# First relational layer of a graph network: the row that is picked on TensorE becomes the last tile of the following, even chunk

## The chip, the cores and the metric

One NeuronCore of a Trainium2 chip runs the whole program. The metric is the device time of one execution in microseconds (us), lower is better. Times given as "median" are medians of separate executions; the rows of the trace come from one profiled execution.

## The reference

The program is a two-block graph network on 3125 nodes of 128 features and 100000 edges that are sorted by destination. The first block is relational (two layers), the second a GCN (two layers); both have a layer norm ahead and a residual around them. Cut to what matters here, a relational layer is:

```python
def _rel_layer(h, src, dst, etype, norm, V, comp, loop_w, bias, activation):
    c = comp[etype]                                   # 8 coefficients an edge
    for b in range(num_bases):                        # 8 bases
        xb = h @ V[b]
        m = m + c[:, b, None] * xb[src]
    m = m * norm
    agg = jax.ops.segment_sum(m, dst, num_segments=h.shape[0])
    out = agg + bias + h @ loop_w
```

Each edge needs the row `h[src]` of its source node, 128 floats, and the sum over the edges of a destination node. That fetch of rows is what the change is about.

## The kernel before, in words

The 100000 edges are cut into 782 tiles of 128 edges, eight tiles to a chunk (`CHUNK`), 98 chunks, four chunks to a group of 128 destination nodes (`CPG`), 25 groups. The first relational layer is "layer 0" in the code (`relational_layer(..., 0, ...)`), the second "layer 1". Both keep the rows of 64 tiles in a ring in SBUF (`ring`, eight chunks of eight tiles). The engines run their own queues, written out by hand and kept together by counting semaphores.

Of layer 0, chunk by chunk:

- **POOL** (GpSimd) gathers the rows of a tile with one indirect DMA (line 854 for chunks 2 to 7, line 831 for the rest), in the order of the tiles. Ahead of a chunk it waits for `edges_done` of the chunk four before (`LEAD`), half way through it for `product_done`. Every gather counts 16 onto `ring_even` or `ring_odd`, by the parity of its chunk; `landings` says how much has come when a chunk is complete, `gathers` how many of its tiles POOL fetches.
- **PE** (TensorE) has in a chunk: `sum_slab` (lines 1180, 1211, 1216, 1219), which waits for DVE's `rel_M` (line 983) and counts the graph's adjacency; 13 or 12 matmuls of the picked row in three parts (`pick_sixth`, line 1280), between them the 16 matmuls of the coefficients (line 483); then `sum_edges` and the eight matmuls of the chunk's tiles (line 1342; each stands as two records in the trace, since it is float32). The third part of the picked row's matmuls stands behind the fourth tile.
- **DVE** (VectorE) builds for each chunk the operands `rel_lo` (978), `rel_C` (993) and `rel_M` (983), the one-hot types of a later chunk (`make_onehot`, 474, two instructions) and the coefficients (489, 494). Once in a group it folds the adjacency into degrees (`fold_degrees`, 1061 to 1063).

One tile in every second chunk is not gathered: it is **picked on PE**. SP loads the 128 source numbers of the tile's edges into `src_row` (`load_sources`), DVE compares them with the node numbers into the one-hot `pick` (`make_pick`, 1016, in two halves), PE multiplies it with the node features, which lie in SBUF as three bf16 parts (`h_parts`), and DVE adds the three parts into the ring's slot (`keep_picked`, 1032), which counts `row_ready`. PE's matmuls of one picked row are spread over two chunks: the first half over an even chunk, the second over the odd chunk behind it. 46 rows are made so, in chunk pairs whose odd chunk is 5 to 95 (`first_picks`). Before the change the row is tile 7 of that same odd chunk, so PE waits for `row_ready` ahead of its last tile (line 1341):

```python
if layer == 0 and i == CHUNK - 1 and j % 2 == 1 and not (isinstance(c, int) and not first_picks(c)):
    pe.wait_ge(row_ready, number(g, j) + 1)
```

On DVE `keep_picked` stands in the queue behind `rel_M` of the *next* (even) chunk and ahead of the second half of the next pick. At the layer's end chunk 96 is followed by the turn of the last group (lines 563 to 565), `sum_slab` and the edges of chunk 97, and two degree sums on DVE (`sum_degrees`, line 1052). Then layer 1 starts, and with it POOL's next gather.

## Time and profile before

| what | value |
|---|---|
| median of 3 executions | 2001.1 us (1999.92 to 2003.72) |
| profiled execution, its own time | 1999.43 us |
| its span in the trace | 1997.8 us |
| layer 0's gathers on POOL end | 978.8 us into the span |
| layer 1's first gather starts | 999.6 us into the span |

Busy shares over the whole span: PE 86%, DVE 75%, POOL 69%, ACT 18%. The page of the profile gives the share of an engine's busy time, and in a second list what each engine waited for; the two differ where an engine has a fixed pause between two instructions, as POOL has here.

### The profile page before, as it was taken

The numbers are of one execution on the slowest core, as the hardware profiler recorded it, in microseconds if no ns is written. First come the engines' busy times: TensorE is split into PE (matmuls) and PEld (weight loads), VectorE is DVE, ScalarE is ACT, GpSimd is POOL, SyncE is SP. The second block draws the span as 40 slices with busy tenths as digits, with TensorE's granted clock in tenths as the row PEclk, the third lists the DMA queues.
The fourth block names the chain that finished last, engine by engine and source line by source line (L and its number), as shares of the span: only waits on it lengthen the run. The fifth ranks groups of instructions, "written<-read, shape, count | busy, mean of one in ns | idle before, by whom it ended". The sixth has DMA issues, their size and how long they took to land. (4 is left out here: it accounts for less than half of the span.)

```text
span 1997.8 us, 41905 instructions
## 1 busy us (share of the span) xinstructions
PE 1727.5 (86%) x12855; PEld 1237.7 (62%) x12856; DVE 1493.0 (75%) x2360; ACT 357.1 (18%) x869; POOL 1383.6 (69%) x1505
## 2 busy tenths in 40 slices
PE   1488888888888888888659999999999999999998
PEld 1366656556556556556537777767667676676564
DVE  7898888888888888887478888877777777652533
ACT  2032222222222222222201011101011010011300
POOL 5777777777777777777477777777777777777000
PEclk8589989889889889988779999999999999989999
DMA  5334334334334334333222222233333322325473
GB/s 151 92 98 114 96 99 109 94 98 110 94 97 108 95 97 109 95 96 88 70 60 64 63 64 64 63 85 86 86 101 93 86 80 80 115 57 167 154 240 120
DMA packets 196506, 196.71 MB, mean 98 GB/s; under 512 B 109132, under 2 KB 160089, under 8 KB 196410
## 3 DMA queue, kind: packets, MB, share of 16 engines
q0 software_dynamic: 45056, 92.36, 18.1%
q1 hardware_dynamic: 143302, 99.03, 17.2%
q10 hardware_dynamic: 8052, 4.04, 0.7%
q8 instruction: 59, 0.97, 0.2%
q14 instruction: 37, 0.30, 0.0%
HBM read 169.75 MB, written 25.57 MB: 98 GB/s over the span
## 5 line engine op out<-in xcount | busy, mean ns | idle before, releaser
L831 POOL DMA_INDIRECT ring<-h_rows,rel_idx x1292 | 1239.8, 960 | 387.9 <-issue 360.2
L1016 DVE TENSOR_TENSOR rel_pick<-rel_src_row,dve_bank 128x1664 bf16<-128x1664 int32 (+1 forms) x268 | 486.2, 1815 | 104.0 <-PE rel_ps_p L1267 56.5
L1342 PE MATMUL rel_ps_z<-rel_C,ring 128*128 128x56 f32 x3100 | 404.1, 278 | 95.2 <-DVE ring L1032 76.3
L1342 PEld LDWEIGHTS rel_ps_z<-rel_C,ring 128*128 128x128 f32 x3100 | 392.1, 197 | 136.6 <-issue 125.8
L1267 PE MATMUL rel_ps_p<-rel_h_parts,rel_pick 128*128 128x384 bf16 x1650 | 283.7, 328 | 24.3 <-DVE rel_h_parts L1004 22.0
L1440 ACT ACTIVATE rel_ZT<-rel_ps_z 128x304 f32 x292 | 114.2, 426 | 1028.6 <-PE rel_ps_z L1342 1023.1
L1280 PE MATMUL rel_ps_p<-rel_h_parts,rel_pick 128*128 128x384 bf16 x1150 | 264.8, 361 | 0.0
L1267 PEld LDWEIGHTS rel_ps_p<-rel_h_parts,rel_pick 128*128 128x128 bf16 x1650 | 158.6, 100 | 138.3 <-issue 30.5
L1430 ACT ACTIVATE rel_A<-rel_ps_a 128x500 f32 x292 | 165.5, 603 | 387.3 <-PE rel_ps_a L1219 209.5
L1219 PE MATMUL rel_ps_a<-rel_M,rel_lo 128*128 128x175 bf16 x784 | 156.3, 299 | 37.1 <-DVE rel_M L983 36.9
L1267 PE MATMUL carried<-rel_h_parts,rel_pick 128*128 128x384 bf16 x1100 | 186.2, 326 | 2.4 <-DVE rel_pick L1016 2.4
L983 DVE TENSOR_TENSOR rel_M<-dve_bank,key_table 128x1400 bf16<-128x1400 f32 x98 | 157.3, 1605 | 0.0
L1267 PEld LDWEIGHTS carried<-rel_h_parts,rel_pick 128*128 128x128 bf16 x1100 | 105.9, 98 | 71.0 <-DVE rel_pick L1016 2.8
L1280 PEld LDWEIGHTS rel_ps_p<-rel_h_parts,rel_pick 128*128 128x128 bf16 x1150 | 113.5, 112 | 56.6 <-issue 22.1
L1219 PEld LDWEIGHTS rel_ps_a<-rel_M,rel_lo 128*128 128x128 bf16 x784 | 77.3, 109 | 105.9 <-issue 61.8
L854 POOL DMA_INDIRECT ring<-h_rows,idx_table x100 | 101.8, 1018 | 56.0 <-issue 33.6
L978 DVE TENSOR_TENSOR rel_lo<-dve_bank,src_lo_table 128x1024 bf16<-128x1024 f32 x98 | 119.4, 1218 | 27.2 <-PE rel_ps_a L1211 27.2
L993 DVE TENSOR_TENSOR rel_C<-dve_bank,coef 128x448 f32<-128x448 f32 x196 | 121.4, 619 | 14.4 <-PE rel_ps_z L1347 2.5
L483 PE MATMUL rel_ps<-comp_parts,rel_onehot 100*128 100x48 bf16 x1568 | 63.3, 193 | 46.3 <-DVE rel_onehot L474 28.6
L483 PEld LDWEIGHTS rel_ps<-comp_parts,rel_onehot 100*128 100x128 bf16 x1568 | 61.2, 103 | 66.1 <-DVE rel_onehot L474 28.8
L474 DVE TENSOR_SCALAR rel_onehot<-rel_types,type_id 100x1024 bf16<-100x1024 bf16 x196 | 91.8, 510 | 10.4 <-DMA rel_types<-edge_types 5.9
L1026 DVE TENSOR_TENSOR rel_pick<-rel_extra_row,dve_bank 128x1664 bf16<-128x1664 int32 (+1 forms) x44 | 79.9, 1816 | 19.6 <-PE carried L1267 19.6
(233 smaller groups left out, 1776.1 us busy)
## 6 DMA issues: line engine op xcount, KB each, us to landing
ring<-h_rows,rel_idx POOLq DMA_INDIRECT x1292
A_slabs<-rel_A SPq DMA_DIRECT2D x25, 800.0 KB
A_slot<-A_slabs SPq DMA_DIRECT2D x25, 800.0 KB, 4.5
rel_types<-edge_types SPq DMA_DIRECT2D x97, 200.0 KB
early_slot<-A_slabs SPq DMA_DIRECT2D x18, 896.0 KB, 6.3
rel_src_row<-in_src_dram SPq DMA_DIRECT2D x134, 64.0 KB, 3.0
last_slot<-A_slabs SPq DMA_DIRECT2D x4, 512.0 KB, 5.5
ring<-h_rows,idx_table POOLq DMA_INDIRECT x116
```

Source lines behind the costliest of these rows:

```text
L483: ins = self.nc.tensor.matmul(self.ps[:, e * 6 * NB:(e + 1) * 6 * NB], self.onehot[:, s, h, e * P:(e + 1) * P], flat(self.t.comp[:, h, :, ...
L831: g_.indirect_dma_start(ring[:, s * CHUNK + i, :], None, rows_in, bass.IndirectOffsetOnAxis(ap=idx[which][:, n:n + 1], axis=0)).then_inc(l ...
L978: v.tensor_tensor(lo[s][:, :, :], lows.unsqueeze(1).to_broadcast(shape), t.src_lo[:, bass.ds(c * CHUNK, CHUNK)].unsqueeze(2).to_broadcast( ...
L983: v.tensor_tensor(M[s][:, :, :], keys.unsqueeze(1).to_broadcast(shape), t.key[:, bass.ds(c * CHUNK, CHUNK)].unsqueeze(2).to_broadcast(shap ...
L993: v.tensor_tensor(C[s][:, :, :, :], match[s].unsqueeze(2).to_broadcast(shape), t.coef[layer][:, bass.ds(first, CHUNK), :].unsqueeze(3).to_ ...
L1016: v.tensor_tensor(pick[:, b0:b0 + n, :], src_row[s][:, :].unsqueeze(1).to_broadcast(shape), node_ids[:, b0:b0 + n].unsqueeze(2).to_broadca ...
L1219: ins = m_.matmul(into[:, :, bass.ds(half_at[h][i], TW)], lo[s][:, h * HALF + i, :], keyed(s, h * HALF + i), start=False, stop=(i == HALF ...
L1267: ins = m_.matmul(ps_p[s][:, 0:3 * P], pick[:, b, :], h_parts[:, b, :, :].rearrange("p c n -> p (c n)"), start=(b == 0), stop=(b == SRC_BL ...
L1280: ins = m_.matmul(ps_p[0][:, 0:3 * P], pick[:, b, :], h_parts[:, b, :, :].rearrange("p c n -> p (c n)"), start=(b == 0), stop=(b == SRC_BL ...
L1342: ins = m_.matmul(bank(ps_z[s], NB)[:, :, bass.ds(at[i], TW)], ring[:, first + i, :], C[s][:, i, :, :], start=False, stop=(i == n - 1))
L1430: ins = s_.activation(A[into][:, :, bass.ds(column, HN)], half_bank(ps_a[h]), ACT.Copy)
L1440: ins = s_.activation(ZT[into][:, :, bass.ds(column, CN)], bank(ps_z[s], NB), ACT.Copy)
```

## The change

In layer 0 the picked row of a pair becomes tile 7 of the *even* chunk behind the pair (6, 8, ... 96) and no longer of the odd chunk that ends it. When the row is made, on which engines and in which order, stays. POOL now gathers eight tiles in odd chunks and seven in even ones; SP loads the source numbers of the later chunk's tile; DVE writes the sum into the later slot; PE waits for `row_ready` in even chunks. Layer 1 is as it was.

```diff
-            return CHUNK if late else CHUNK - (1 if layer == 1 else s % 2)
+            return CHUNK if late else CHUNK - (1 if layer == 1 else 1 - s % 2)
...
-            if layer == 0 and s % 2 == 1:
-                return half * (CHUNK * 16) if isinstance(half, int) and half < 3 else half * (gathers(s) * 16) + 2 * 16
-            return half * (gathers(s) * 16)
+            if s % 2 == 0:
+                return half * (CHUNK * 16) if isinstance(half, int) and half < 3 else half * (gathers(s) * 16) + 3 * 16
+            return half * (CHUNK * 16)
...
-                for i in range(c * CHUNK, c * CHUNK + (CHUNK if layer == 0 and c < 4 else gathers(c))):
+                for i in range(c * CHUNK, c * CHUNK + (CHUNK if layer == 0 and c < FIRST_PICK else gathers(c))):
...
-                    sp.dma_start(src_row[s][:, :], rows[:, bass.ds((g * CPG + (CPG + j)) * (CHUNK * P) + (CHUNK - 1) * P, P)].to_broadcast([P, P]))\
+                    sp.dma_start(src_row[s][:, :], rows[:, bass.ds((g * CPG + (CPG + j + 1)) * (CHUNK * P) + (CHUNK - 1) * P, P)].to_broadcast([P, P]))\
...
-                                keep_picked(number(*behind), 0, (parity * CPG + j - 1) % SLOTS_RING * CHUNK + CHUNK - 1)
+                                keep_picked(number(*behind), 0, (parity * CPG + j) * CHUNK + CHUNK - 1)
...
-                        if layer == 0 and i == CHUNK - 1 and j % 2 == 1 and not (isinstance(c, int) and not first_picks(c)):
-                            pe.wait_ge(row_ready, number(g, j) + 1)
+                        if layer == 0 and i == CHUNK - 1 and j % 2 == 0 and not (isinstance(c, int) and not first_picks(c - 1)):
+                            pe.wait_ge(row_ready, (number(g, 1) if j == 2 else number(g - 1, 3)) + 1)
```

The queues of DVE, ACT and SP hold the same instructions in the same order. On PE, in the tiles of an odd chunk of the loop (lines with `-` are of before, with `+` of the change; the matmul that follows is the chunk's last tile):

```order
 L1342 ISA
 L1342 MATMUL rel_ps_z<-rel_C,ring 128x8x7
-L1341 REGISTER_ALU
-L1342 ISA [waits rel0_row_ready]
+L1342 ISA
 L1342 MATMUL rel_ps_z<-rel_C,ring 128x8x7
 L1180 MATMUL rel_ps_z<-zero 128x304 [waits rel0_zt_kept]
```

The wait for the picked row is gone from the odd chunk. In the even chunk of the same loop it has come:

```order
 L1342 ISA
 L1342 MATMUL rel_ps_z<-rel_C,ring 128x8x7
-L1342 ISA
+L1341 ISA
+L1342 ISA [waits rel0_row_ready]
 L1342 MATMUL rel_ps_z<-rel_C,ring 128x8x7
 L1180 MATMUL rel_ps_z<-zero 128x304 [waits rel0_zt_kept]
```

It stands ahead of that chunk's last tile, one chunk later in the queue. On POOL, one odd chunk and the even chunk behind it, before:

```order
L831 DMA ring<-h_rows,rel_idx 128x128 [waits ring_odd]
L831 DMA ring<-h_rows,rel_idx 128x128 x3
L715 REGISTER_ALU
L831 DMA ring<-h_rows,rel_idx 128x128 [waits rel0_product_done]
L831 DMA ring<-h_rows,rel_idx 128x128 x2
L715 REGISTER_ALU
L715 ISA [waits rel0_edges_done]
L715 REGISTER_ALU [waits ring_even]
L803 ISA [waits rel0_idx_ready]
L803 COPY rel_idx<-idx_table 128x32
L831 DMA ring<-h_rows,rel_idx 128x128 x4
L715 REGISTER_ALU
L831 DMA ring<-h_rows,rel_idx 128x128 [waits rel0_product_done]
L831 DMA ring<-h_rows,rel_idx 128x128 x3
```

And in the changed kernel:

```order
L831 DMA ring<-h_rows,rel_idx 128x128 [waits ring_odd]
L831 DMA ring<-h_rows,rel_idx 128x128 x3
L715 REGISTER_ALU
L831 DMA ring<-h_rows,rel_idx 128x128 [waits rel0_product_done]
L831 DMA ring<-h_rows,rel_idx 128x128 x3
L715 REGISTER_ALU
L715 ISA [waits rel0_edges_done]
L715 REGISTER_ALU [waits ring_even]
L803 ISA [waits rel0_idx_ready]
L803 COPY rel_idx<-idx_table 128x32
L831 DMA ring<-h_rows,rel_idx 128x128 x4
L715 REGISTER_ALU
L831 DMA ring<-h_rows,rel_idx 128x128 [waits rel0_product_done]
L831 DMA ring<-h_rows,rel_idx 128x128 x2
```

The odd chunk has 4 + 4 gathers in place of 4 + 3, the even one 4 + 3 in place of 4 + 4; the pair has 15 both times, and no wait is added or taken away.

## Rows read from the trace of the kernel before

**Rows 1.** Layer 0's loop. Columns: stretch, length, busy us and instructions (x) of each engine, granted TensorE clock, DMA share, GB/s.

```profile
100.00:979.00 879.00, 733.27 (x6065) 537.25 (x6064) 721.53 (x1109) 230.00 (x500) 674.56 (x719) 0.90 0.39 99
```

**Rows 2.** Waits of POOL, 100 to 1000 us: who waited for whom, us in total, times, longest.

```profile
POOL ring L831 <- issue: 190.1, 639, 0.3
POOL ring L854 <- POOLq L662: 20.8, 1, 20.8
```

**Rows 3.** Groups by line, POOL's gathers, 100 to 979 us: count, busy us, mean ns, idle before.

```profile
L831 POOL DMA_INDIRECT ring<-h_rows,rel_idx x674 | 655.2, 972 | 200.7 <-issue 190.1 <-DMA ring<-h_rows,rel_idx 8.8 <-PE rel_ps L483 0.9
```

**Rows 4.** Waits of PE, 100 to 979 us.

```profile
PE rel_ps_z L1342 <- DVE ring L1032: 76.3, 46, 3.6
PE rel_ps_a L1219 <- DVE rel_M L983: 33.4, 22, 1.8
...
PE rel_ps_z L1342 <- DMA ring<-h_rows,rel_idx: 9.9, 9, 3.3
```

**Rows 5.** Waits of PE for landings alone, 880 to 1000 us.

```profile
PE rel_ps_z L1342 <- DMA ring<-h_rows,rel_idx: 8.8, 4, 3.3
```

**Rows 6.** Timeline of POOL at the end of layer 0: start us, us, what, idle before it.

```profile
960.39 0.94 POOL L831 DMA_INDIRECT ring<-h_rows,rel_idx  x1 [0.30 <-issue]
961.64 0.94 POOL L831 DMA_INDIRECT ring<-h_rows,rel_idx  x1 [0.30 <-issue]
...
970.37 0.94 POOL L831 DMA_INDIRECT ring<-h_rows,rel_idx  x1 [0.30 <-issue]
...
977.86 0.94 POOL L831 DMA_INDIRECT ring<-h_rows,rel_idx  x1 [0.30 <-issue]
999.60 0.94 POOL L854 DMA_INDIRECT ring<-h_rows,idx_table  x1 [20.80 <-POOLq L662]
```

**Rows 7.** Timeline of PE around one wait for the picked row, odd chunk.

```profile
405.01 0.42 PE L1342 MATMUL rel_ps_z<-rel_C,ring 128*128 128x56 f32 x2 [3.22 <-DVE ring L1032]
...
406.09 0.95 PE L1219 MATMUL rel_ps_a<-rel_M,rel_lo 128*128 128x175 bf16 x4
...
412.32 0.99 PE L1342 MATMUL rel_ps_z<-rel_C,ring 128*128 128x56 f32 x8
```

**Rows 8.** Timeline of DVE, the same wait.

```profile
402.74 1.60 DVE L983 TENSOR_TENSOR rel_M<-dve_bank,key_table 128x1400 bf16<-128x1400 f32 x1
404.26 0.54 DVE L1032 TENSOR_REDUCE ring<-rel_ps_p 128x128 f32<-128x384 f32 x1
```

**Rows 9.** Groups by line, DVE's `rel_M`, one for each chunk, 100 to 979 us.

```profile
L983 DVE TENSOR_TENSOR rel_M<-dve_bank,key_table 128x1400 bf16<-128x1400 f32 x95 | 152.5, 1605 | 0.0
```

**Rows 10.** Timeline of PE at the end of layer 0: chunk 95's tiles, its wait, chunk 96's tiles.

```profile
962.97 1.07 PE L1342 MATMUL rel_ps_z<-rel_C,ring 128*128 128x56 f32 x8
...
967.19 0.42 PE L1342 MATMUL rel_ps_z<-rel_C,ring 128*128 128x56 f32 x2 [1.90 <-DVE ring L1032]
...
973.03 3.63 PE L1342 MATMUL rel_ps_z<-rel_C,ring 128*128 128x56 f32 x16 [3.10 <-DMA ring<-h_rows,rel_idx]
```

**Rows 11.** Timeline of POOL, three gathers that took longer.

```profile
415.98 1.15 POOL L831 DMA_INDIRECT ring<-h_rows,rel_idx  x1 [0.30 <-issue]
...
948.42 1.60 POOL L831 DMA_INDIRECT ring<-h_rows,rel_idx  x1 [0.30 <-issue]
950.32 1.02 POOL L831 DMA_INDIRECT ring<-h_rows,rel_idx  x1 [0.30 <-issue]
```

**Rows 12.** Timeline of DVE at the same times.

```profile
415.29 1.02 DVE L474 TENSOR_SCALAR rel_onehot<-rel_types,type_id 100x1024 bf16<-100x1024 bf16 x2
...
948.25 1.96 DVE L1061 TENSOR_TENSOR rel_A<-rel_A 128x1536 f16<-128x1536 f16 x3
```

**Rows 13.** Groups by line, POOL's gathers in layer 1, 1100 to 1700 us.

```profile
L831 POOL DMA_INDIRECT ring<-h_rows,rel_idx x479 | 453.2, 946 | 142.2 <-issue 130.7 <-DMA ring<-h_rows,rel_idx 6.4 <-PE rel_ps_p L1267 2.1
```

**Rows 14.** Two stretches of layer 0's end, columns as in the first group.

```profile
973.00:983.00 10.00, 9.04 (x39) 8.46 (x39) 5.08 (x1) 1.21 (x4) 4.58 (x5) 0.50 0.52 123
...
985.00:992.00 7.00, 5.33 (x40) 4.82 (x38) 0.42 (x2) 1.91 (x4) 0.00 (x0) 0.92 0.49 118
```

## The prediction

> **What bounds the kernel now.** I read four views, in this order. The stretches first: in layer 0's loop PE is busy 733 of 879 us and DVE 722, so neither is full, and POOL with 675 looks the idlest of the three [rows 1]. The list of waits corrects that. POOL's idle time in layer 0 is 639 pauses of 0.3 us between one gather and the next that end on nothing, and then a single long wait of 20.8 us at the end [rows 2]. A gather takes 0.94 us and the pause 0.30, and this repeats every 1.25 us without a break until 978.8 [rows 6]. POOL is therefore the engine that never stops in layer 0, though its busy share is the lowest. Third, PE's own waits: 76.3 us in 46 pieces for the picked row, 33.4 us for `rel_M`, and only 9.9 us for landed rows [rows 4]. Nearly all of that last sum, 8.8 us in four pieces, lies after 880 us [rows 5]. So for most of the layer the rows are there long before PE wants them, and at the end they are not. The counts say the same: from 100 to 979 us DVE has built 95 chunks [rows 9] while POOL has gathered 674 + 12 tiles, 686 / 7.5 = 91.5 chunks. PE and DVE eat up a lead of 3.5 chunks, about 3.5 x 9.6 = 34 us, and reach POOL near the end. Fourth, the end itself: chunk 96's last gather is the one that starts at 970.37, and PE, idle for 3.10 us, starts its tiles at 973.03, that is 2.7 us after that start [rows 6, 10]. Everything up to layer 1's first gather at 999.60 hangs on this, 26.6 us later.
>
> **The change, part by part.**
>
> *The wait taken out of the odd chunks.* It costs PE 76.3 us in 46 places [rows 4], two in a group: a long one and a short one. What it is worth even to PE is less. In the long one PE stood from 405.01 - 3.22 = 401.79 [rows 7]. Without it, it does the last tile and what lies up to the first matmul that needs `rel_M`, 406.09 - 405.01 = 1.08 us, and is there at 402.87. But `rel_M` is finished only at 402.74 + 1.60 = 404.34 [rows 8]. PE waits there some 1.5 us and begins at about 404.4 in place of 406.09: of 3.2 us, 1.7 is gained and 1.5 changes its name. With one such place in a group, PE and DVE gain about 1.7 us a group, some 40 us over 23 groups if nothing else bounds them. On the path that sets the end it is worth **0**: what hides it is POOL's row of gathers, which ends at 978.8 whether PE is early or not. If that cover were gone, it would be worth those 40 us. What is late next is the landing: PE and DVE lose 34 us of lead in 24 groups now, 1.4 us a group, and would lose 1.4 + 1.7 = 3.1, so they reach POOL after 34 / 3.1 = 11 groups, in the middle of the layer, and stand at landings from there on.
>
> *The wait put into the even chunks.* The row is in the ring at 404.26 + 0.54 = 404.80 [rows 8]; the even chunk that now uses it has its tiles before those of 412.32 [rows 7], and its last tile some 7 us after the row. Price 0. Behind it on PE stand the clearing of the bank and the next `sum_slab`; the same row is asked for earlier in that chunk already, ahead of the next pick's matmuls, as it was before. One register instruction comes to PE's queue, nothing to DVE's.
>
> *The gather that changes chunk.* POOL issues 46 fewer than there are tiles before (odd chunks 5 to 95) and after (even chunks 6 to 96): 736 in the layer both times, with the same copies and waits between them. Term 0. An odd chunk is complete one gather later, 1.25 us; an even one at the same gather as before, since 7 + 8 and 8 + 7 are both 15. Chunk 95's last gather is then the one of 961.64 and not that of 960.39 [rows 6]; with 2.7 us to PE its tiles start at 964.3 in place of 962.97, and save the wait of 1.90 behind them [rows 10]. PE is done with that chunk 0.6 us earlier and stands for chunk 96 until 973.03 as before. Term 0.
>
> *SP.* The same loads at the same places, of the numbers 1024 edges further on. Term 0. *Layer 1* is untouched: 0.
>
> *The layer's end.* The 26.6 us from 973.03 to 999.60 hold the same instructions. PE runs the first ten at a granted clock of 0.50, the 1.2 GHz level, since it stood ahead of them, and is back at 2.4 GHz (0.92 in the mean) from about 985 [rows 14]. It will stand there at least as long again, so I take 0. If the clock came back a stretch sooner or later, it would be worth some 2 us: chunk 96's tiles took 3.63 us, against 0.99 for half of them at the high level, so 1.6 of it is the clock [rows 7, 10].
>
> *The length of a gather.* This is the one term that the change can move without meaning to. 674 gathers take 655.2 us [rows 3]; at 0.94 each it would be 633.6, so 21.6 us of layer 0, 0.9 us a group, is stretch. In layer 1 the mean is 946 ns, hardly any [rows 13]. The stretched ones lie beside two sorts of DVE work that only layer 0 has: a pair of one-hots from 415.29 on and a gather of 1.15 at 415.98; the fold of the degrees from 948.25 on, and gathers of 1.60 and 1.02 [rows 11, 12]. How much is lost depends on where such an instruction falls in the 1.25 us of a gather. Before, DVE's course slides past POOL's, by about 1.4 us a group, so all positions occur and 0.9 us is their mean. Where PE waits for landings, DVE follows POOL in a fixed position, and the 12 groups behind the meeting point repeat one case. Bounds for a group: nothing, or (four pairs at 0.21, one fold at 0.66 + 0.08) 1.6 us. That is -0.9 to +0.7 a group, over 12 groups **-11 to +8 us**. No row says which, so I take the mean, 0.
>
> Sum: 0 against the profiled execution's 1999.4 us (span 1997.8 and 1.6 around it), which lies 1.7 us under the median of 2001.1. I predict the median, rounded, **2001.0 us**. No difference under 0.2%, 4 us, can be told from no change here.
>
> **Rivals.**
>
> *A. The gathers fall better.* The stretch in the second half of the layer shrinks by over a third of a microsecond a group: -4 to -11 us, 1990 to 1997. For it: most positions in a gather seem to cost little, since the mean pair costs less than the 0.21 of the row shown. Against it: nothing picks the good ones. Chance 0.15.
>
> *B. The gathers fall worse, and it gets slower.* The same mechanism at the other end: fold and one-hots of DVE, now in step with POOL, meet the sensitive part of a gather in every group. Price up to 8 us, 2009. It decides from +0.33 us a group on (4 us over 12 groups). The gathers of 948.42 and 950.32 already stand in the stretch where PE waits for landings, and lost 0.74 us to one fold. Chance 0.12. The Trainium skill would make this one much dearer: its page "SBUF — State Buffer", section "SBUF: two separate sides", says that VectorE in a two-port mode holds the port pair that it shares with GpSimd, and that GpSimd cannot write descriptors for a DMA until VectorE is done. By that rule the fold's 1.96 us and eight one-hots of 0.51 would be lost in full when they coincide, about 6 us a group and up to 60 us in all. The rows agree with the direction but not with the size: beside a fold of 1.96 us the gathers lost 0.74.
>
> *C. PE and DVE bound the layer after all.* Then the 40 us come in: about 1961. Against it stand the unbroken gathers. Chance 0.03.
>
> *D. The change does not take the wait out.* The rows of the queues show it moved, but DVE could now be waited for at `rel_M` for the whole amount; PE's idle time would only change its name. The time is the same, 2001; it is part of the forecast's case.
>
> **How the numbers follow.** Forecast and D 0.70, A 0.15, B 0.12, C 0.03. Faster by over 4 us: A and C, 0.18. Slower: B, 0.12. The likeliest case alone gives 1997 to 2005. For 8 in 10 the range goes on to most of A and B, without their far ends and without C: 1993 to 2007.
>
> **What would show it.** Right: PE's waits for DVE's `ring` (line 1032) in layer 0 fall from 76 us to under 5; those for `rel_M` rise from 33 to 50 or more; those for landings rise from 10 to 40 or more and begin before 600 us. POOL's last gather of the layer ends between 970 and 987, its gathers keep their 0.3 us pauses, and from there to layer 1's first gather it is 20.8 us again, within 2. The mean of line 831 in layer 0 tells A from B: under 965 ns is A, over 980 is B. Wrong: POOL's gathers end far earlier than 970, or long pauses for `edges_done` or `product_done` appear among them, or layer 1 (its first gather to the end, 998 us) changes by more than 2 us.

## The result, and the profile after

| | before | changed | difference |
|---|---|---|---|
| median of 20 executions each, us | 2000.28 (1996.44 to 2003.72) | 2002.72 (1999.37 to 2008.04) | ratio 1.0015, 95% interval 1.0008 to 1.0021 |
| profiled execution, us | 1999.43 | 2005.3 | +5.9 |
| its span, us | 1997.8 | 2003.6 | +5.8 |
| start of POOL's last gather of layer 0 | 977.86 | 980.35 | +2.49 |
| from there to layer 1's first gather | 21.7 | 22.0 | +0.2 |
| layer 1's first gather to the end | 998.2 | 1001.3 | +3.1 |

The change costs 0.15%: less than the 0.2% that the prediction counted as a difference, but the interval leaves out 1. It rests on this one comparison; no later run repeats the two kernels side by side near 2000 us. The predicted 2001.0 is 1.7 us low and the range holds the time. The profiled execution of the changed kernel is 2.6 us above its own median, so its +5.8 overstates the loss of +2.4. The same wait list as in [rows 4], PE in the changed kernel, 100 to 985 us (total us, times, longest):

```profile
PE rel_ps_z L1342 <- DMA ring<-h_rows,rel_idx: 69.6, 44, 4.2
PE rel_ps_a L1219 <- DVE rel_M L983: 47.2, 32, 2.6
PE rel_ps_h L563 <- ACT rel_ZT L1440: 17.2, 24, 0.8
PE rel_ps L483 <- DVE coef L494: 8.8, 31, 0.8
```

The 76.3 us for the picked row are gone. `rel_M` rose from 33.4 to 47.2 and the landed rows from 9.9 to 69.6: the removed idle time came back under two other names, and a third, the coefficients (`coef`), rose from 0.8 to 8.8. PE's waits between 360 and 420 us show where the landings begin; from 300 to 360 there is none:

```profile
PE rel_ps_a L1219 <- DVE rel_M L983: 6.0, 3, 2.2
PE rel_ps_z L1342 <- DMA ring<-h_rows,rel_idx: 2.9, 2, 2.1
```

POOL's waits of the changed kernel, 100 to 1010 us, and its group of gathers, 100 to 979 us (busy us, mean ns, idle before them), which answer to [rows 2, 3]:

```profile
POOL ring L831 <- issue: 187.6, 625, 2.1
POOL ring L854 <- POOLq L662: 21.0, 1, 21.0
POOL ring L831 <- DMA ring<-h_rows,rel_idx: 10.4, 34, 0.3
```

```profile
L831 POOL DMA_INDIRECT ring<-h_rows,rel_idx x671 | 653.0, 973 | 201.6 <-issue 186.9 <-DMA ring<-h_rows,rel_idx 10.4 <-PE rel_ps_z L1347 3.7
```

A gather is 973 ns long in place of 972: no stretch came or went. The row that matters is the first one's last number, 2.1: one pause was not 0.3 us long. POOL's timeline shows it, and the layer's end (start, us, what, idle before):

```profile
337.59 0.94 POOL L831 DMA_INDIRECT ring<-h_rows,rel_idx  x1 [0.30 <-issue]
340.61 0.94 POOL L831 DMA_INDIRECT ring<-h_rows,rel_idx  x1 [2.08 <-issue]
...
980.35 0.94 POOL L831 DMA_INDIRECT ring<-h_rows,rel_idx  x1 [0.30 <-issue]
1002.32 0.94 POOL L854 DMA_INDIRECT ring<-h_rows,idx_table  x1 [21.03 <-POOLq L662]
```

That pause is 1.8 of the 2.5 us by which layer 0's gathers end later. No code was being loaded then: the queues that load instructions start nothing between 281 and 904 us of this trace. PE's timeline at the end is the picture of [rows 10]: chunk 96 starts 2.45 us later, after 3.97 us of idle time:

```profile
975.48 3.63 PE L1342 MATMUL rel_ps_z<-rel_C,ring 128*128 128x56 f32 x16 [3.97 <-DMA ring<-h_rows,rel_idx]
```

One more thing changed that the prediction did not look at, PE's clock while it waits for landings (stretch, length, busy time of PE, PEld, DVE, ACT and POOL, PE's clock, DMA share, GB/s), before first, then changed:

```profile
360.00:979.00 619.00, 513.11 (x4196) 373.73 (x4195) 499.21 (x761) 160.80 (x350) 474.79 (x507) 0.90 0.38 98
```

```profile
360.00:979.00 619.00, 509.43 (x4139) 386.28 (x4139) 491.70 (x754) 156.31 (x340) 475.02 (x506) 0.88 0.38 97
```

Over the whole program the clock was 0.911 to 0.921 in the 20 executions of the changed kernel; the kernel before had 0.924 in its profile and 0.922 to 0.927 in 22 later executions near 2000 us. POOL covers what this costs PE in layer 0.

In layer 1, whose code the change leaves alone, 1.1 us came between its first and last gather (848.4 to 849.5) and 2.0 behind the last (149.8 to 151.7, before rounding 149.76 to 151.74). Of the latter, the same 21 matmuls of line 1193, before first, then changed:

```profile
1845.65 4.70 PE L1193 MATMUL carried<-early_slot,hp_parts 128*128 128x512 f16 x21
```

```profile
1840.05 4.69 PE L1193 MATMUL carried<-early_slot,hp_parts 128*128 128x512 f16 x21
1849.46 6.29 PE L1193 MATMUL carried<-early_slot,hp_parts 128*128 128x512 f16 x21
```

The instructions and their number are alike, one burst is 1.59 us longer. The granted clock goes with it (columns as above), before first, then the changed kernel:

```profile
1845.50:1850.30 4.80, 4.80 (x26) 2.31 (x27) 1.39 (x5) 1.38 (x4) 2.84 (x3) 1.00 0.19 50
```

```profile
1846.00:1849.00 3.00, 2.03 (x19) 2.04 (x19) 0.89 (x3) 0.32 (x2) 2.39 (x3) 1.00 0.49 135
1849.00:1852.00 3.00, 3.00 (x11) 1.31 (x10) 1.39 (x5) 1.46 (x4) 2.08 (x4) 0.54 0.17 44
1852.00:1856.00 4.00, 4.00 (x21) 1.99 (x20) 0.05 (x1) 0.00 (x0) 0.78 (x1) 0.92 0.16 33
```

It fell to the 1.2 GHz level for some 3 us in the changed kernel and stayed at 2.4 GHz before. In both PE had just been idle ahead of line 1372, for 1.34 us in the changed kernel and 1.23 us in before.

### The profile page after: what moved, and what is told of

The parts are those of the page before. It is cut to its first block and busy times, and to the rows that moved or that the text cites. A ratio compares the mean times of both kernels' runs of the same rounds, so it can differ in the third digit from the quotient of the medians.

```text
span 2003.6 us, 41914 instructions
## 1 busy us (share of the span) xinstructions
PE 1729.1 (86%) x12855; PEld 1255.2 (63%) x12856; DVE 1489.3 (74%) x2360; ACT 356.1 (18%) x869; POOL 1384.3 (69%) x1505
## 3 DMA queue, kind: packets, MB, share of 16 engines
q0 software_dynamic: 45056, 92.36, 18.5%
q1 hardware_dynamic: 143302, 99.03, 17.3%
## 5 line engine op out<-in xcount | busy, mean ns | idle before, releaser
L1342 PE MATMUL rel_ps_z<-rel_C,ring 128*128 128x56 f32 x3100 | 411.6, 285 | 77.9 <-DMA ring<-h_rows,rel_idx 72.1
L1342 PEld LDWEIGHTS rel_ps_z<-rel_C,ring 128*128 128x128 f32 x3100 | 406.7, 204 | 114.5 <-issue 104.1
L1219 PE MATMUL rel_ps_a<-rel_M,rel_lo 128*128 128x175 bf16 x784 | 139.2, 291 | 50.8 <-DVE rel_M L983 50.4
```

Of the source, the lines that this page charges most:

```text
L1219: ins = m_.matmul(into[:, :, bass.ds(half_at[h][i], TW)], lo[s][:, h * HALF + i, :], keyed(s, h * HALF + i), start=False, stop=(i == HALF ...
L1342: ins = m_.matmul(bank(ps_z[s], NB)[:, :, bass.ds(at[i], TW)], ring[:, first + i, :], C[s][:, i, :, :], start=False, stop=(i == n - 1))
```

## The experiments

**The numbers need one remark.** Each set of experiments had the kernel before run beside it. In the first five sets it took 2584 to 2618 us (here called the long condition), and in the last two 2000 and 2003, though one chip served in a set of either kind. So every ratio below is to the kernel before of the same set, and what the runs show of the long condition is told as that. The words "layer 0" with a number mean the time from the gather at 54 us to the layer's last.

### The change alone, and its faster PE undone

`b_again` is the kernel before as a kernel of its own, `a_again` and `a_third` are the changed kernel. `e1_wait_kept`, twice, is the changed kernel with PE's old wait beside the new one:

```diff
+                        if layer == 0 and i == CHUNK - 1 and j % 2 == 1 and not (isinstance(c, int) and not first_picks(c)):
+                            pe.wait_ge(row_ready, number(g, j) + 1)
                         if layer == 0 and i == CHUNK - 1 and j % 2 == 0 and not (isinstance(c, int) and not first_picks(c - 1)):
```

> The kernel before once more, for a second trace. All theories: 2000.3 us, ratio 1.000. Theory S (stretch): the gathers of the first layer, 24.0 us longer than 0.94 us each in the first trace, are so again within 1.5 us. Theory P (single pauses and ends): POOL's gathers end 978 us into the span as before, and no single pause over 1 us stands among them. Theory N (chance between builds and runs): the pieces of the time differ from the first trace as much as those of the changed kernel do, 2 us or so each.

> The changed kernel once more. Theory S: ratio 1.0015 again, and the gathers' stretch in the first layer is larger than in the kernel before by 2 to 3 us (it was 24.3 against 24.0 in the first pair of traces, which speaks against it). Theory P: the single pause of 2.1 us at 340 us, which stood among the gathers with no wait of the program before it, is there again at the same gather, and POOL ends 2.5 us later than before. Theory N: the pause is gone or elsewhere, and the ratio lies nearer to 1.000.

> The changed kernel with the old wait put back: PE waits for the picked row ahead of the last tile of the odd chunk too, though it uses it in the even chunk. Leaves nothing of the computation out. Gathers, landings and source loads are those of the change, PE's pace that of before. Theory S (PE in step with POOL lengthens gathers or waits): the loss goes, 2000.3 us, ratio 1.000, and PE's waits for landings in the first layer are under 20 us. Theory L (the odd chunk complete one gather later costs time by itself): ratio 1.0015 or more, with landing waits at odd chunks. Theory N: anything from 0.999 to 1.002.

> The changed kernel on another chip, after one on which every kernel took 2540 to 2584 us, with pauses between instructions on all engines. If this chip is like the first (before near 2000 us): Theory S, 1.0015 again, gathers' stretch in the first layer 26 us or more. Theory P, the pause of 2.1 us at 340 us again at the same gather, POOL's last gather of the layer near 980.4. Theory N, no pause at that place and a ratio between 0.999 and 1.002.

> The changed kernel with the old wait for the picked row put back ahead of the odd chunk's last tile (it is no longer needed there). Nothing of the computation is left out. Where before takes near 2000 us: Theory S, the loss goes, ratio 1.000. Theory L (odd chunks complete one gather later), ratio 1.0015 or more. Theory N, 0.999 to 1.002. All: POOL's gathers stay unbroken and the layer ends within 3 us of 978.8.

| kernel | median, us | ratio to before | 95% | layer 0, us |
|---|---|---|---|---|
| b_again | 2583.6 | 1.0006 | 0.9984 to 1.0028 | 1190.9 |
| a_again | 2541.2 | 0.9843 | 0.9808 to 0.9879 | 1141.8 |
| e1_wait_kept | 2556.8 | 0.9906 | 0.988 to 0.9931 | 1167.8 |
| a_third | 2567.2 | 0.9828 | 0.9786 to 0.9871 | 1166.9 |
| e1_wait_kept_2 | 2584.0 | 0.9892 | 0.9851 to 0.9932 | 1181.8 |

In the long condition the same change wins 1.6 to 1.7%, and with the old wait kept it still wins 0.9 to 1.1%. Where both have a profile (`b_again` and `a_again`) layer 0 is 49 us shorter and the total 42. Theories S, L and N were about the loss near 2000 us, so these five kernels do not decide between them. Theory P's sign did come: `a_again` has the single pause ahead of the same gather,

```profile
416.82 1.00 POOL L831 DMA_INDIRECT ring<-h_rows,rel_idx  x1 [2.16 <-issue]
```

and `a_third` and both `e1_wait_kept` have it with 2.06 to 2.23 us; `b_again` has 0.30 there. In this condition POOL does not bound the layer. The waits of the kernel before there (`b_again`, 300 to 900 us), where [rows 2] have none but the 0.3 us pauses ("remote" marks a wait whose end has no instruction in the trace):

```profile
ACT rel_A L1430 <- remote: 154.9, 23, 12.4
POOL ring L831 <- issue: 135.1, 323, 6.5
...
POOL ring L831 <- remote: 71.1, 35, 3.2
```

POOL is 45 us ahead of PE at chunk 10 and still 40 at chunk 94 (in the first profile 26 and 6.5), and it pauses for PE and not the other way round. What PE waits for there is in the last section.

### Fewer gathers: is there a gain behind POOL?

Two of the eight gathers of a layer 0 chunk are left out from chunk 8 on, in the kernel before and in the changed one, so that POOL cannot be the bound:

```diff
+                    if layer == 0 and i in (2, 3):
+                        continue
                     n = start * CHUNK + i
```

(`landings` counts two fewer.) The kernels were run in both conditions.

> Leaves out two gathers (tiles 2 and 3) of every chunk from the eighth on in the first layer, in the kernel before; the ring keeps older rows there, so the sums of these edges are of other rows. 180 gathers fewer of 1.25 us: POOL alone would end the layer 225 us sooner, so PE and DVE bound it. Forecast's theory (POOL's gathers bound the layer, PE and DVE hold 34 us less): the layer runs at PE's and DVE's pace of 9.33 us a chunk, measured where they were not held up, 98 chunks: some 20 to 25 us under before, 1975 to 1981. Rival (PE and DVE bound it already): 2000.

> The same two gathers left out of every chunk from the eighth on, in the changed kernel; the same edges get other rows. Forecast's theory: the gain that POOL hides comes out. PE and DVE run at 9.07 us a chunk where they were not held up (chunks 10 to 28 of the changed kernel's trace), 0.26 us a chunk less than before: 22 to 26 us under e2_light_before, near 1953. By the prediction's own term, 1.7 us a group, 40 us under it. Rival (the wait only changed its name at the building of rel_M): within 5 us of e2_light_before.

> Two gathers of every chunk from the eighth on left out in the first layer of the kernel before (older rows stay in the ring and are summed in their place), once more, now timed. Forecast's theory on a chip where before takes near 2000 us: 1975 to 1981. On one where before takes near 2600 us, as in the last two calls: 2382 again within 1%, since POOL waits there for PE and DVE already in the full kernel and fewer gathers help only layer 1's start and what the gathers held up. Rival (PE's and DVE's pace has nothing to do with the gathers): ratio 1.00 to before in the second case.

> The same with the changed kernel, other rows summed for the same edges. Near 2000 us for before: 22 to 26 us under e2_light_before_2. Near 2600: 1.5 to 2% under it, as the full kernels differ there (0.984 and 0.983). Rival (the change gains only through the gathers): the same time as e2_light_before_2.

> The kernel before with two of layer 0's eight gathers left out of each chunk from chunk 8 on (columns of other rows are read in their place, so other rows are summed). If the chip is in the condition of the first times (the kernel before near 2000 us), POOL's gathers no longer bound layer 0 and TensorE does: at 9.33 us a chunk, as this kernel's chunks 10 to 28 ran while unheld, the 96 chunks take some 26 to 30 us less than by POOL's pace, so 1970 to 1981 us in all. If the kernel before takes near 2600 us, 0.91 of it, as the same kernel gave at that pace.

> The changed kernel with the same two gathers left out. With the kernel before near 2000 us: the wait on the kept row is gone and POOL holds nothing, so the change's gain is no longer hidden. By the pace of the unheld chunks (0.26 us a chunk) it is 22 to 26 us under e7_light_before; by my term of 1.7 us a group, about 40 us. If the loss of 0.15% came from TensorE's own work in layer 0 and not from POOL, the gain would be missing or small. With the kernel before near 2600 us: 0.98 to 0.99 of e7_light_before.

| kernel | median, us | ratio to before | 95% |
|---|---|---|---|
| e2_light_before (one run) | 2381.7 | | |
| e2_light_after (one run) | 2335.8 | | |
| e2_light_before_2 | 2380.6 | 0.9095 | 0.9065 to 0.9125 |
| e2_light_after_2 | 2353.0 | 0.8978 | 0.893 to 0.9026 |
| e7_light_before (before 2002.54) | 1992.15 | 0.995 | 0.9935 to 0.9966 |
| e7_light_after | 1958.62 | 0.9783 | 0.9769 to 0.9798 |

In the long condition the light kernel before came as expected (2382 within 1%), and the light changed one is 1.2% under it in `e2_light_after_2`, less than the 1.5 to 2% expected; the single runs had 1.9%.

The pair e7 is the test of the prediction's main argument. With POOL's cover gone the change is worth 1992.15 - 1958.62 = **33.5 us**; with it, -2.4. PE's waits in `e7_light_before`, 100 to 985 us:

```profile
PE rel_ps_z L1346 <- DVE ring L1036: 75.8, 46, 3.5
PE rel_ps_a L1223 <- DVE rel_M L987: 36.8, 24, 1.9
```

and in `e7_light_after`:

```profile
PE rel_ps_a L1223 <- DVE rel_M L987: 91.8, 47, 2.6
```

The waits for the row and for `rel_M` are nearly those of [rows 4], and in the changed kernel they become 91.8 us of `rel_M`: 55 of the 75.8 us changed their name. Another 7.3 us came back as waits for `coef` (0.8 in the one, 8.1 in the other), so some 13.5 are gone. None comes back as landings. DVE's `rel_M` counts the chunks (count, first and last start, us), light before and light changed, 200 to 850 us:

```profile
L987 DVE TENSOR_TENSOR rel_M<-dve_bank,key_table x69: 1596/1601/1606, 208.3 to 844.5; 128x1400 bf16<-128x1400 f32 x69
```

```profile
L987 DVE TENSOR_TENSOR rel_M<-dve_bank,key_table x73: 1596/1603/1606, 204.3 to 849.7; 128x1400 bf16<-128x1400 f32 x73
```

636.2 / 68 = 9.36 us a chunk against 645.4 / 72 = 8.96: 0.39 a chunk, 1.57 a group. The waits name only 0.6 of this a group (13.5 us over 23). The rest is in PE's busy time. From the `sum_slab` of chunk 12 to that of chunk 92, 80 chunks or 20 groups, with the same 5205 matmul records, light before and light changed (columns as above):

```profile
195.65:940.35 744.70, 621.64 (x5205) 451.94 (x5204) 611.50 (x951) 193.39 (x420) 432.89 (x470) 0.91 0.33 87
```

```profile
191.64:905.11 713.47, 604.23 (x5205) 443.89 (x5204) 607.68 (x952) 191.73 (x420) 441.19 (x469) 0.93 0.35 91
```

Of the 31.2 us, 13.8 are idle time (744.70 - 621.64 against 713.47 - 604.23), 0.7 a group, and 17.4 are busy time, 0.9 a group: the same matmuls take less time. The clock, 0.93 in place of 0.91, goes with a part of that. It is not all: from chunk 12 to 34 the clock is 0.92 in both, and the busy time falls from 167.17 to 164.27 us, 0.5 a group. That the missing break ahead of each odd chunk's last tile does this is likely, but no run shows it by itself. This is the opposite of the full kernels, where the changed one ends in waits for landings and has the lower clock.

My expectation for `e7_light_before` alone, 1970 to 1981, missed. I had counted PE's 9.33 us a chunk, 26 to 30 us less than POOL's pace gives, over all 96 chunks; but PE starts behind POOL and in the kernel before meets it only at the end [rows 5]. Taking POOL's bound away can then give only what PE waits for landings, 9.9 us [rows 4], and it gave 10.4. The expectation for `e7_light_after`, 22 to 26 us or 40 below it, had the truth between its two figures.

### The wait alone, out and in

`e3_no_wait` is the kernel before with PE's wait removed: the picked row is made as before but kept in a buffer of its own, and POOL gathers all eight tiles. `e4_more_wait` is the kernel before with the changed kernel's wait added.

```diff
-                        if layer == 0 and i == CHUNK - 1 and j % 2 == 1 and not (isinstance(c, int) and not first_picks(c)):
-                            pe.wait_ge(row_ready, number(g, j) + 1)
...
+                into = kept_row[:, :] if layer == 0 else ring[:, slot, :]
```

```diff
+                        if layer == 0 and i == CHUNK - 1 and j % 2 == 0 and not (isinstance(c, int) and not first_picks(c - 1)):
+                            pe.wait_ge(row_ready, (number(g, 1) if j == 2 else number(g - 1, 3)) + 1)
```

> The kernel before with the wait for the picked row taken out of the odd chunks and nothing else of the change: the row is still made, but into a buffer of its own, and the last tile of each odd chunk from 5 to 95 is summed from an older row of the ring, so these edges get other rows. Two gathers more than before (chunks 5 and 7). Together with e1 (gathers moved, wait kept) it splits the change. Forecast's theory (all that the change gives is the wait): near 2000 us for before, no difference, 1.000 to 1.001; near 2600, where POOL waits for PE and DVE, the whole gain of the changed kernel, 0.983 to 0.984. Rival (the gathers' new places count, as e1's 0.989 to 0.991 says): 0.990 to 0.995.

> The kernel before with the change's new wait in the even chunks added: PE asks for a count that was reached a chunk before. Nothing of the computation is left out, and no gather moves; PE's queue has the instructions of the changed kernel plus the old waits, as in e1. Forecast's theory: 1.000 in any condition, since the wait is long over. Rival (where the instructions lie in PE's queue costs or gives time by itself): in e1's direction, 0.99.

Measured, in the long condition: `e3_no_wait` 2582.78 us, ratio 0.9882 (0.985 to 0.9914), layer 0 1177.0; `e4_more_wait` 2618.27, 1.0009 (0.9983 to 1.0035). The new wait's price of 0 stands. `e3_no_wait` lies between its two theories (0.983 to 0.984 and 0.990 to 0.995), so neither has all of it. The old wait's removal is worth 1.2% there by itself, moving the gathers by itself 1.0% (`e1_wait_kept`), both together 1.6 to 1.7%: they overlap. Why moving one gather from an even chunk to an odd one should win anything with the old wait in place is not settled.

### More gathers: POOL made dearer

Three more gathers of half rows a chunk from chunk 8 on, into a spare buffer, in both kernels:

```diff
+                    if layer == 0 and i < 3:
+                        g_.indirect_dma_start(spare[:, s % 2 * 3 + i, :], None, rows_in.rearrange("n (a d) -> (n a) d", a=2),
+                                              bass.IndirectOffsetOnAxis(ap=idx[which][:, n:n + 1], axis=0)).then_inc(landed, 16)
```

> The kernel before with three gathers more in every chunk from the eighth on in the first layer, of half rows into a buffer that nobody reads; the computation is whole. POOL then issues 10.5 gathers a chunk, 13.1 us at 1.25 us each, against the 12.1 us a chunk that the layer took in b_again (1191 us for 98 chunks). Forecast's theory (a row of gathers without a break bounds the layer): the layer's gathers take 924 + 270 x 1.25 = 1261 us, 70 us more than in b_again, total near 2690 where before takes 2617; POOL's pauses over 0.7 us nearly vanish. Rival G (each gather by itself slows PE, as the light kernels' 2380 us hint: 180 gathers fewer gave 237 us): 270 more cost 350 us, total near 2970, and POOL still pauses.

> The changed kernel with the same three gathers more a chunk. Forecast's theory: with POOL the bound again the change gives nothing, ratio to e5_heavy_before 1.000 within 0.002, though it gives 1.6 to 1.7% on the same sort of chip without the extra gathers. Rival G, and any theory by which the change's gain does not depend on POOL: 1.0 to 1.7% under e5_heavy_before.

Measured, long condition: 2985.47 us, 1.1411 (1.1391 to 1.1431), and 2953.23, 1.13 (1.1277 to 1.1323). The changed one is 1.1% under the other, 32 us. Both numbers are rival G's (near 2970, and 1.0 to 1.7%) and not the forecast's theory's (near 2690, and 1.000). Had POOL's gathers been a plain bound as in the first profile, nothing should be left of the gain; so in this condition they are not. Their number still goes with the time: 270 more gathers cost 370 us, 180 fewer save 236, 1.3 to 1.4 us each either way.

### Pauses put into POOL

POOL waits in each chunk, ahead of its third tile, until the chunk's first two have landed:

```diff
+                    if layer == 0 and i == 2:
+                        hold(pool, landed, landings(m * (SLOTS_RING // 2) + s // 2, s, late) + 2 * 16)
```

> The kernel before with one more stop of POOL in every chunk of the first layer: ahead of the third tile it waits until its own first two gathers of the chunk have landed. Nothing else changes, nothing is left out. In b_again, of PE's counts that rose later than the record of the matmul ended, 202 of 285 rose while POOL was pausing over 0.6 us, though it paused only 26% of the time. Theory V (on these chips PE's counts get through when POOL pauses, so each gather in an unbroken row is paid for by whoever waits for PE): more pauses let PE's counts through sooner; POOL's own pace is 7.5 x 1.25 + 1.7 = 11.1 us a chunk, layer 0's gathers 1090 us in place of 1190, total 70 to 120 us under before. Rival (POOL's row only costs its own time, or chance): the stop is 1.7 us a chunk more on a loop that is full, or nothing: 0 to 160 us over before. On a chip with before near 2000: 9.4 + 1.7 against 9.4 us, some 130 to 160 us over before.

> The changed kernel with the same stop. Theory V: 70 to 120 us under the changed kernel without it (2567 on the second chip), and 1 to 2% under e6_pause_before if PE and DVE still bound the layer, equal to it if POOL now does. Rival: 0 to 160 us over the changed kernel.

Measured beside 2000.48: 2219.54 us, 1.1102 (1.1083 to 1.112), and 2238.06, 1.1188 (1.1169 to 1.1208). POOL's waits, 100 us to the layer's end, before's form first, then the changed one's:

```profile
POOL ring L833 <- DMA ring<-h_rows,rel_idx: 248.7, 89, 5.1
```

```profile
POOL ring L833 <- DMA ring<-h_rows,rel_idx: 266.0, 90, 6.3
```

Idle time on POOL goes into the total in full: these waits stand in place of 89 pauses of 0.3 us, so they add 248.7 - 27 = 222 us, and the total rose by 219. POOL bounds the layer here. Theory V was made for the long condition and is not tested by this; the figure given for a chip near 2000 us, 130 to 160 us over before, missed, because a stop costs 2.5 us (222 / 89) and not the 1.7 that I had counted. And the change loses 0.8% where POOL waits for its own landings, where equal times were expected: 17.3 of the 18.5 us are longer waits for them, of nearly the same number. PE waits for landings in both, for 191.5 us in the one and 258.4 in the other. Why a landing comes later in the changed order is not shown.

### The old wait kept, beside 2002.54

> The changed kernel, its gathers and its new rows as they are, but with TensorE's old wait on the kept row also kept in the odd chunks, so that it has the old pace while unheld. With the kernel before near 2000 us: if the 0.15% that the change lost comes from TensorE reaching POOL's landings earlier (a faster unheld pace, then work in shorter pieces), it goes: 0.999 to 1.001. If it comes from where the gathers or the rows stand, it stays: 1.001 to 1.002. With the kernel before near 2600 us: 0.989 to 0.991.

Measured: 2004.13 us, 1.0006 (0.9994 to 1.0018). The interval holds 1.000 and 1.0015 alike, so the run does not decide between the theories that it was made for. Its profile helps more. PE waits for the row again (`DVE ring` 64.1 us), and yet POOL's timeline has the single pause in the same place, longer:

```profile
339.34 0.95 POOL L831 DMA_INDIRECT ring<-h_rows,rel_idx  x1 [0.30 <-issue]
345.08 0.95 POOL L831 DMA_INDIRECT ring<-h_rows,rel_idx  x1 [4.80 <-issue]
```

So it is in `e6_pause_after`:

```profile
400.27 0.94 POOL L833 DMA_INDIRECT ring<-h_rows,rel_idx  x1 [1.98 <-issue]
```

It is one and the same gather in all three, number 237 of the program. In the profiles of the old order, of before and of `e6_pause_before`, that gather has its 0.30. With the profiles of the long condition it is seven out of seven in the new order (1.98 to 4.80 us) against none out of five in the old one (before, `b_again`, `e3_no_wait`, `e4_more_wait`, `e6_pause_before`). So it goes with the new order of gathers and not with PE's pace. But the new order is not alone in having such a pause. With the number of gathers changed, the old order has it too. In `e7_light_before`:

```profile
414.92 0.94 POOL L835 DMA_INDIRECT ring<-h_rows,rel_idx  x1 [2.18 <-issue]
```

This is gather 242; gathers 352 and 462 have 2.18 as well, and in `e7_light_after` gathers 237, 347 and 457 do, each 110 gathers (20 chunks) behind the last. So the change moved where such a pause falls, or let one show; what makes it no record names.

## Why the prediction was right or wrong

- **The size of the change on the path, "Sum: 0", failed by 2.4 us** (1.6 to 4.2 by the interval): no change was forecast, and the kernel got slower. Two terms of the sum were set at nothing and were not nothing. *The gather that changes chunk*, "term 0": the number of gathers is equal, as I said, but one of them starts 1.8 us late (1.7 to 1.9 in five of the other six profiles of that order with all gathers, 4.5 in the sixth). On a path that POOL bounds this goes into the total in full. *Layer 1*, "untouched: 0", and my own bound for it, 2 us, was passed with 3.1. Its profile puts 1.6 of them into one burst of matmuls at its end. That this belongs to the change is not shown: `e7_wait_kept`, in the new order too, has 4.70 us for that burst, and of the five long bursts in these profiles three are of the old order. From the last gather to the end the seven profiles taken beside 2000 us, each of another kernel, have 149.8, 149.7 and 155.1 us in the old order and 151.7, 153.1, 149.9 and 150.9 in the new. That spread is larger than the loss, and so is the 7.3 us from the fastest to the slowest of the 20 executions before. The pause is thus the one part of the loss that repeats. How the 2.4 us divide between it and the rest stays open.
- **What bounds the kernel** was right. POOL's gathers cover the gain, and without them it is there. That the light changed kernel takes 1958.6 us, where rival C had been priced at 1961, is luck in part: 10.4 of the difference come from taking the cover away and 33.5 from the change.
- **"1.7 is gained and 1.5 changes its name", about 1.7 us a group and some 40 us over 23 groups:** 1.57 a group, and 33.5 us in all, where nothing hides it. The figure is nearly right, but not by its own working. It was idle time alone, and of idle time only 0.7 a group went; the other 0.9 are matmuls that take less time, a term that the prediction did not have. The share that changes its name was larger than for the one place that I read: 73% against 47%, and 7.3 us more at `coef`. In the kernel itself, while PE is still unheld, the pace shows less: from 104 to 373 us DVE starts 31 `rel_M` before and 32 after, 8.96 and 8.70 us apart, 1.0 a group. That is the stretch and not POOL: the light pair has 8.98 and 8.71 there. It is why the 0.26 us a chunk in my expectations was too low.
- **The lead** was to be used up after 11 groups. Landings begin between 360 and 420 us, about chunk 34, in the ninth group. The marks "0 for line 1032", "over 40 for landings, before 600 us" and "970 to 987" all came; `rel_M` was to reach 50 and stopped at 47.2; it reaches 91.8 only in the light kernel, where no waits for landings take its place. The mark "its gathers keep their 0.3 us pauses" failed at one gather.
- **The wait put in: 0**, shown by `e4_more_wait`, though only in the long condition.
- **The stretch of the gathers, rivals A and B:** -11 to +8 us was the widest term of the sum, and the mean moved by 1 ns, 0.7 us over the layer. The two rivals took 0.27 of the chance and most of the range, and neither came. The changed kernel was slower, but not by B's mechanism. The lock by the Trainium skill's page "SBUF — State Buffer", section "SBUF: two separate sides", which would have made B dear, is not seen at the size that the prediction worked out from it: 6 us a group would be 0.2 us on each of 30 gathers, and from chunk 34 on, where DVE follows POOL, no such thing shows in the mean of 973 ns over the layer. (Six us over 12 groups would also be 72 us and not 60.)
- **The layer's end, "I take 0",** held: from POOL's last gather to layer 1's first 21.7 us became 22.0. The clock was looked at only there; that it would be lower in all of the layer's second half (0.88 in place of 0.90) was not foreseen, and POOL covers it.
- **The chance of 0.70 for "within 0.2%"** was the right case, and the number 2001.0 was within 0.1%. What it missed is that 20 executions tell 0.15% apart.

## What to carry to other kernels

A wait removed from an engine that another one covers gives back its time as the next waits in the queue, and the wait list says how it splits. It can also shorten the busy time of the engine, which the wait list does not show: count length, idle and busy time over the same chunks. The gain that is hidden is best priced by making the covering engine lighter in both kernels, which here turned -2.4 us into 33.5. Taking the cover away from one kernel only gives what the other engine now waits for it, not the difference of the paces. And a term of 0 for code that is not touched is good only to what its own timing scatters by from profile to profile: here up to 5 us of a 150 us stretch, more than the effect looked for.

## What the runs showed of the hardware

**The same program, 29 to 31% longer.** In five sets of runs the kernel before took 2584 to 2618 us in place of 2000, and this was no property of a chip, since one of them gave 2584 and later 2000. POOL's and DVE's instructions are as long as before (a gather 966 ns on average, `rel_M` 1.61 us), but what they wait for comes late, and PE's clock is 0.82 over the span in place of 0.92. DVE and PE in `b_again`:

```profile
592.24 1.89 DVE L1016 TENSOR_TENSOR rel_pick<-rel_src_row,dve_bank 128x1664 bf16<-128x1664 int32 x1 [7.08 <-remote]
```

```profile
595.35 3.76 PE L563 MATMUL rel_ps_h<-V,rel_ZT 128*128 128x128 f32 x16 [8.60 <-ACT rel_ZT L1440]
```

and POOL beside them:

```profile
591.44 0.94 POOL L831 DMA_INDIRECT ring<-h_rows,rel_idx  x1 [0.30 <-issue]
598.03 0.94 POOL L831 DMA_INDIRECT ring<-h_rows,rel_idx  x1 [5.65 <-issue]
```

I compared the end of each counting matmul with the moment at which its semaphore rose, 150 to 1100 us. In the profiles of before and after all 728 and 726 rose within 0.1 us. In `b_again` 285 of 528 rose later, by up to 8 to 14 us and many at once, and 202 of the 285 rose while POOL was pausing, though it paused a quarter of the time; in `a_again` 200 of 277, at 21%. The recorded rises of DVE's and ACT's counts all lie within 0.15 us of an instruction's end, but in this condition some two fifths of them have no record, so this is shown only for the rest. It looks as if PE's counts are held up while POOL issues gathers, and 1.3 us for each gather fits, but that is argued, not shown. There is a plain rival: POOL waits for PE's counts, so a count that is late finds POOL pausing, whatever made it late. What is shown is that POOL's pauses alone do not make it: in `e6_pause_before` and `e7_light_after` POOL paused 23% of the time, and of 609 and 764 counts none was late. What puts a chip into this condition was not found. It turns the verdict on the change round: 1.6 to 1.7% faster there, 0.15% slower here.

**A clock that falls beside unchanged work.** In the seven profiles of kernels taken beside 2000 us, nearly all bursts of 21 matmuls of line 1193 with 512 columns (1195 or 1197 in kernels with added lines) took 4.69 to 4.86 us; five took 6.2 to 7.2. They stand in either order of gathers: one in the changed kernel and one in `e6_pause_after`, one in `e6_pause_before` and two in `e7_light_before`, of which this is the second:

```profile
1806.45 6.33 PE L1197 MATMUL carried<-early_slot,hp_parts 128*128 128x512 f16 x21 [0.34 <-DVE early_sums L1051]
1817.21 4.71 PE L1197 MATMUL carried<-early_slot,hp_parts 128*128 128x512 f16 x21
```

Its clock was 0.50 from 1806.5 to 1809 us. Here PE had been idle for 2.59 and 1.25 us within the 14 us before, in the changed kernel for 1.34. In before it was idle for 1.23 us at the same place and the clock stayed up. What decides between the two is named by no row.
